# Opening the self attentions in parts between the last passes of the cross attentions

## The reference

```python
x = x + _L0_xattn_ref(_layernorm(x), ctx_512, Wq, Wkv, Wo)        # 16 heads of 16, over the context
x = x + _L0_attn_ref(_layernorm(x), w_attn, b_attn, w_proj, ...)  # causal, 16 heads, over 64 tokens
x = x + _L0_ffn_ref(_layernorm(x), w_gate, w_up, w_down)          # weights rounded to -1, 0, 1
x = x + _L1_xattn_ref(_layernorm(x), ctx_512, ctx_512, ...)       # one head over the context
x = x + _L1_attn_ref(_layernorm(x), W, b)                         # causal, 16 heads, no projection
x = x + _L1_ffn_ref(_layernorm(x), gate_w, ...)                   # 32 experts, top 8, and a shared one
```

## Time and profile before

| | |
|---|---|
| profiled execution, device time | 1285.13 us |
| its span (first to last instruction) | 1283.0 us |
| instructions | 30312 |
| TensorE matmuls busy | 1197.6 us (93%) |
| VectorE, ScalarE, GpSimd busy | 810.0, 643.5, 558.5 us |
| layer 1 ends, layer 2 begins | 250 to 281 us from the start |
| layer 2 ends, feed-forward begins | 400 to 414 us |
| layer 4 ends, layer 5 begins | 564 to 579 us |

### The profile page before, as it was taken

How to read it: one execution, slowest core, us unless ns; L and a number is a source line. 1 busy time by engine, 2 the same in 40 slices (tenths; PEclk the granted TensorE clock), 3 DMA queues, 4 the chain that set the end, 5 groups by cost and what they waited for, 6 DMA issues and landing times.

```text
span 1283.0 us, 30312 instructions
## 1 busy us (share of the span) xinstructions
PE 1197.6 (93%) x9820; PEld 946.3 (74%) x9828; DVE 810.0 (63%) x1773; ACT 643.5 (50%) x1394; POOL 558.5 (44%) x833
## 2 busy tenths in 40 slices
PE   6899999989997777998998999999999999999998
PEld 5677777767775445877776888888888888888886
DVE  4688888757776885658999875444444544444444
ACT  5766666634454786545556443334334433343342
POOL 2244444467775443548887433333233223323322
PEclk9999999989999998999999999999999999999999
DMA  8200000000000000210000133333333343333331
GB/s 286 59 18 16 16 16 8 2 1 2 0 0 18 16 0 10 74 30 14 1 0 1 54 108 120 114 110 106 109 103 114 121 128 103 110 114 114 105 112 62
DMA packets 34041, 80.13 MB, mean 62 GB/s; under 512 B 4416, under 2 KB 12096, under 8 KB 33984
## 3 DMA queue, kind: packets, MB, share of 16 engines
q1 hardware_dynamic: 32800, 78.09, 18.7%
q10 hardware_dynamic: 1184, 1.31, 0.3%
HBM read 77.03 MB, written 2.36 MB: 62 GB/s over the span
## 4 chain that ended last, share of the span: by engine, by line
PE 79%; DVE 7%; issue 5%; ACT 5%; POOL 4%; DMA 0%; ACTq 0%; DVEq 0%; POOLq 0%; SPq 0%
PE ps L2117 10%; PE ps L2119 10%; PE ps L2118 10%; PE ps L2200 5%; PE ps L2199 5%; PE ps L2201 5%; PE ps L421 4%; PE ps L968 3%; PE ps L436 3%; PE ps L409 3%; PE ps L959 2%; PE ps L938 2%; PE ps L975 2%; PE ps L947 2%; POOL Sm L1212 1%
## 5 line engine op out<-in xcount | busy, mean ns | idle before, releaser
L2486 POOL TENSOR_TENSOR sw<-sg,wb 128x512 f32<-128x512 f32 x136 | 176.4, 1297 | 386.7 <-ACT sg L2310 352.8
L2389 DVE TENSOR_TENSOR a<-sw,ps 128x512 f32<-128x512 f32 x136 | 93.5, 687 | 224.8 <-POOL sw L2486 224.5
L2315 ACT ACTIVATE ah<-a 128x512 fp32r<-128x512 f32 x136 | 86.0, 632 | 290.7 <-DVE a L2389 268.5
L2117 PE MATMUL ps<-Hh,wh 128*128 128x512 f32 x544 | 215.3, 396 | 0.0
L2118 PE MATMUL ps<-Hl,wh 128*128 128x512 f32 x544 | 214.4, 394 | 0.0
L2119 PE MATMUL ps<-Hh,wl 128*128 128x512 f32 x544 | 214.4, 394 | 0.0
L2393 DVE TENSOR_TENSOR al<-a,ah 128x512 fp32r<-128x512 f32 x136 | 95.5, 702 | 62.5 <-ACT ah L2315 59.3
L674 ACT ACTIVATE Pr<-ps,mx 128x256 f32<-128x256 f32 x256 | 103.9, 479 | 61.1 <-DVE mx L575 61.1
L2119 PEld LDWEIGHTS ps<-Hh,wl 128*128 128x128 f32 x544 | 101.8, 187 | 25.1
L2117 PEld LDWEIGHTS ps<-Hh,wh 128*128 128x128 f32 x544 | 101.9, 187 | 24.8 <-issue 0.8
L2118 PEld LDWEIGHTS ps<-Hl,wh 128*128 128x128 f32 x544 | 101.9, 187 | 23.6
(11 more groups left out here) (238 smaller groups left out, 2469.1 us busy)
## 6 DMA issues: line engine op xcount, KB each, us to landing
wb<-token_weights SPq DMA_DIRECT2D x64, 512.0 KB, 3.7
raw<-in_ew SPq DMA_DIRECT2D x66, 384.0 KB, 3.0
cT<-in_ctxT SPq DMA_DIRECT2D x16, 256.0 KB, 2.7
cx<-in_ctxT SPq DMA_DIRECT2D x15, 256.0 KB, 2.7
X<-in_x SPq DMA_DIRECT2D x1, 1536.0 KB, 7.2
wqkv<-in_wqkv SPq DMA_DIRECT2D x2, 768.0 KB, 5.1
raw3g<-in_wg SPq DMA_DIRECT2D x1, 1024.0 KB, 5.5
raw3u<-in_wu SPq DMA_DIRECT2D x1, 1024.0 KB, 7.6
```

Source lines behind the costliest of these rows:

```text
L2117: eng.matmul(ps[:, bank, :], wh[:, u, w], HhT[:, c, cols], start=(c == 0), stop=False)
L2389: eng.tensor_tensor(a[:, tt, :], sw[:, tt, :], ps[:, UB[tt], :], ALU.mult).then_inc(m_a, 1)
L2486: eng.tensor_tensor(sw[:, tt, :], sg[:, tt, :], wb[:, u, tt * UT:(tt + 1) * UT], ALU.mult).then_inc(m_sw, 1)
```

## The change

`long_pipeline` and `routed_pipeline` take a `first` and a `finish`, which are generators: they yield `PART` between pieces. `in_turn` changes over between the running block's `finish` and the next block's `first` at each such yield. Computed values and the number of operations stay the same. The rest is order:

- Both cross attentions get a `finish` on each engine, both self attentions a `first`. The first `scores` and the second `qkproj` of the self attention move ahead of the last operations of the cross attention, and `mask(0,0)` ahead of its last `add_x`.
- `opened` is split: each piece waits only for the banks that it uses. In layer 2 the transpose of pair 0 goes to bank 7 (`F0`) instead of bank 3.
- The normalisation of the next block's pair 0 is done in pass 14 (`leading`) instead of 15, in layer 1 and layer 2; so are the two scaled biases.
- GpSimd rounds the last three weight shares (13, 14, 15) in one piece behind pass 14, ahead of the opening.
- In `cross_single`, ScalarE now does `turned(14)`, then the opening's `ln_act`, then `mixed(13)` and `exps(15)`.

```diff
 def in_turn(eng, *layers):
     programs = [layer(eng) for layer in layers]
-    next(programs[0])
+    while next(programs[0]) != MAIN:
+        pass
     for this, following in zip(programs, programs[1:]):
-        next(this)
-        next(following)
+        while next(this) != TAIL:
+            pass
+        mark = next(following)
         for _ in this:
-            pass
+            if mark != MAIN:
+                mark = next(following)
+        while mark != MAIN:
+            mark = next(following)
...
# cross_heads, tensor
+        def finish():
+            i, u, v = NPAIR - 1, 1, 0
+            mix(i - 1, v, 2)
+            turn(i - 1, 7)
+            yield TAIL
+            turn(i, 0)
+            mix(i - 1, v, 3)
+            turn(i, 1)
+            mixed(i - 1)
+            turn(i, 2)
+            scores(i, u, 1)
+            turn(i, 3)
+            mix(i, u, 0)
+            yield PART
+            turn(i, 4)
+            mix(i, u, 1)
+            tail2(i - 1, v)
+            turn(i, 5)
+            tail3(i - 1, v)
+            turn(i, 6)
+            yield PART
+            mix(i, u, 2)
+            turn(i, 7)
+            yield PART
+            mix(i, u, 3)
+            mixed(i)
+            yield PART
+            tail2(i, u)
+            tail3(i, u)
...
# cross_heads, vector: pass 15 as before without the ln_dve calls, then
+            yield TAIL
+            add_x(i - 1)
+            turned(i, 6)
+            yield PART
+            turned(i, 7)
+            yield PART
+            denominators(i)
+            normalise(i, u)
+            yield PART
+            add_x(i)
...
# cross_heads, gpsimd
+            for t in range(NPAIR - 3, NPAIR):
+                quantise(t)
+            yield TAIL
...
# self_heads, tensor
+        def first():
             if layer == 2:
                 eng.wait_ge(s_w1, late)
-                eng.wait_ge(g["c_exp"], 8 * NPAIR)
                 eng.wait_ge(g["c_ke"], 2 * NPAIR)
                 eng.wait_ge(g["c_ve"], 2 * NPAIR)
             else:
+                eng.wait_ge(g["d_qe"], 2 * NPAIR)
+            ln_pe(eng, L, 0, 0, F0)
+            yield PART
+            if layer == 5:
+                eng.wait_ge(g["d_ce"], NPAIR)
+            qkproj(0, 0)
+            yield PART
+            if layer == 2:
+                eng.wait_ge(g["c_exp"], 8 * NPAIR - 1)
+            else:
                 eng.wait_ge(ln_hT, g["lnt"][3] + NPAIR)
-                eng.wait_ge(g["d_qe"], 2 * NPAIR)
-                eng.wait_ge(g["d_ce"], NPAIR)
+            vproj(0, 0)
+            yield PART
+            if layer == 2:
+                eng.wait_ge(g["c_exp"], 8 * NPAIR)
+            ln_pe(eng, L, 1, 1, FH)
+            yield PART
+            if layer == 5:
                 eng.wait_ge(g["d_exp"], NPAIR)
+            scores(0, 0, 0)
+            qkproj(1, 1)
...
# self_heads, vector
+        def first():
+            ln_dve(eng, L, 1, 1)
+            yield PART
+            ln_dve2(eng, L, 1, 1)
+            yield PART
+            v_out(0, 0)
+            yield PART
+            mask(0, 0)
...
# self_heads, scalar
+        def first():
+            eng.wait_ge(s_w1, late)
+            eng.wait_ge(g["s_bq"], 2)
+            ln_act(eng, L, 0, 0, F0)
+            yield PART
+            qk_out(0, 0)
+            yield PART
+            ln_act(eng, L, 1, 1, FH)
...
# cross_single, tensor
+        def finish(body):
+            scores(last, 1, last % R, last // R)
+            mix(last - 2, 1)
+            yield TAIL
+            keys(last, last % R)
+            turn(last - 1, 0)
+            vproj(last - 2, 1)
+            yield PART
+            body(NPAIR, 0, NPAIR // R)
+            yield PART
+            yield PART
+            mix(last, 1)
+            yield PART
+            vproj(last, 1)
...
# cross_single, scalar
+        def finish(body):
+            turned(last - 1, 0)
+            yield TAIL
+            mixed(last - 2, 1)
+            exps(last, 1)
+            yield PART
+            mixed(last - 1, 0)
+            turned(last, 1)
+            yield PART
+            mixed(last, 1)
```

More of the change, by code:

```diff
@@ L55, in opening, with leading @@
     return isinstance(i, int) and i == -1
+def leading(i):
+    return isinstance(i, int) and i == NPAIR - 2
 def closing(i):
@@ L65, in upto, with long_pipeline @@
     return min(n, most) if isinstance(n, int) else n
-def long_pipeline(eng, body, once=None):
-    body(-1, 1, True, False, False, False, 1)
-    yield
+MAIN, TAIL, PART = "main", "tail", "part"
+def long_pipeline(eng, body, first=None, finish=None, once=None):
+    if first:
+        yield from first()
+    else:
+        body(-1, 1, True, False, False, False, 1)
+    yield MAIN
     body(0, 0, True, True, False, False, 1)
@@ L561, in weight_sums @@
             eng.wait_ge(q_sc, 1)
-        yield from long_pipeline(eng, body, weight_sums)
+        yield from long_pipeline(eng, body, finish=finish, once=weight_sums)
     def vector(eng):
@@ L664, in vector @@
         eng.memset(g["epsc"][:, :], EPS).then_inc(s_half, 1)
-        yield from long_pipeline(eng, body, weight_scales)
+        yield from long_pipeline(eng, body, finish=finish, once=weight_scales)
     def scalar(eng):
@@ L992, in body @@
             v = 1 - u
-            if mid:
+            if mid and not known(i, 1):
                 scores(i, u, 0)
@@ L998, in body @@
                 turn(i - 1, v, 1)
[L999 to L1002, removed]
+            if known(i, 1):
                 settled(eng)
-            if front:
+            if front and not known(i, 1):
                 qkproj(i + 1, v)
@@ L1030, in tensor @@
             g["tail5"]["tensor"] = dict(turn=turn, pv=pv)
-        yield from pipeline(eng, body)
+        yield from pipeline(eng, body, first)
     def vector(eng):
@@ L1109, in body @@
                 ln_dve(eng, L, i + 2, u)
-            elif closing(i) and proj:
-                ln_dve(eng, L + 1, 0, v)
-            elif not closing(i) and not proj:
+            elif leading(i) and proj:
+                ln_dve(eng, L + 1, 0, u)
+            elif leading(i):
                 g["first_low"](eng, 0)
@@ L1595, in pairs @@
                 body(R * j + R + r, r, j + 1)
-        for i in range(12, NPAIR):
+        for i in range(12, NPAIR - 1):
             body(i, i % R, i // R)
-        yield
-        for i in range(NPAIR, NPAIR + 3):
-            body(i, i % R, i // R)
+        yield from finish(body)
     def sync(sp):
@@ L1763, in body @@
                 keys_out(i, u)
-        yield from pairs(eng, body)
+        def finish(body):
+            body(last, last % R, last // R)
+            yield TAIL
+            body(NPAIR, 0, 4)
+            yield PART
+            yield PART
+            body(NPAIR + 1, 1, 4)
+            yield PART
+            body(NPAIR + 2, 2, 4)
+        yield from pairs(eng, body, finish)
     def scalar(eng):
```

117 lines of the change are left out of this document (82 added, 35 removed).

## The result

The changed kernel takes 1284.49 us (median of 20 runs, 1280.79 to 1287.15) beside 1287.32 for the kernel before in the same comparison (20 runs). The ratio is 0.9965, with a 95% interval of 0.9952 to 0.9978: 4.5 us less, between 2.8 and 6.2. That ratio is one of means (1288.27 and 1283.75 us); the medians are 2.8 us apart. The sum had said 6.6 us less. The profiled execution took 1282.41 us (span 1280.3), 2.7 less than the one before it.

What follows compares the result with a forecast made beforehand. The prediction took TensorE, busy 93% of the span, as the bound, with waits and half clock at block transitions. Gains 5.5 + 0.8 + 0.3 = 6.6 us from 1286.99 gave 1280.4 us, range 1276.6 to 1284.2.

Steps and rivals of the forecast that it cites:

- The sum: All terms together: 5.5 + 0.8 + 0.3 = 6.6 us less, giving 1280.4 us.
- TensorE's chain of layer 1→2: TensorE's work and remaining waits put layer 2's `scores(0,1)` at 273.8 against 280.77: 7.0 us earlier, the upper end.
- The late chain that decides: Layer 2: last `add_x`, pair 2's statistics, `h`, then second mask at about 276.0 against 281.50; 5.5 us taken as gain.
- Pass 14: Layer 1: the normalisation moved into this pass costs VectorE 0 to 0.1 us.
- Weight slices: GpSimd's last three weight shares, rounded sooner, end near 260; between -0.2 and 0.5 us, taken as 0.
- Layer 4→5: Second mask of layer 5 at 578.4 against 579.19, despite a 1.1 us wait before `vproj(13)`; gain 0.8 us (-1 to 2.6).
- Layer 2→FFN: Layer 2 to feed-forward: last mask no longer waits for GpSimd and rounded `r` comes sooner; gain 0.3 us (0 to 1.0).
- the clock: First transition: about 13.7 us of matmuls in 16, denser than before, so no fall counted on; kept as a risk.
- the clock falls once more: Rival: a fall in one of the merged stretches costs 3 to 4 us, 1283.4 to 1284.4 us; chance 0.18.

Runs made afterwards that it cites:

- e_lns: Changed kernel with pair 2's statistics moved ahead of the cross attention's last `add_x` on VectorE, in both self attentions; 1279.97 us, ratio 0.9931.
- e_qlead: Kernel before with the last three weight shares rounded in one piece and pair 0's normalisation in pass 14, no merging; 1286.98 us, ratio 0.9997.
- e_quant: Kernel before with GpSimd's weight shares 14 and 15 put ahead of the opening of layer 2; 1294.55 us, ratio 1.0045.
- e_first: Changed kernel with only layer 1 to 2 merged, layer 4 to 5 in the order of before; 1284.34 us, ratio 0.9966.
- after: The changed kernel with the whole change, against the kernel before; 1284.49 us, ratio 0.9965.
- e_after2: The changed kernel measured once more, unedited, on another chip than the two half-change runs; 1284.06 us, ratio 0.9968.
- e_second: Changed kernel with only layer 4 to 5 merged, layer 1 to 2 in the order of before; 1291.03 us, ratio 1.0010.
- e_filler: Changed kernel with 13 unread matmuls added on TensorE at layer 2's end and the feed-forward's start; 1279.59 us, ratio 0.9947.
- e_qlate: Changed kernel with weight shares 14 and 15 put back behind the opening of layer 2 on GpSimd; 1286.62 us, ratio 0.9985.
- e_mixed: Changed kernel with ScalarE's old order in layer 4's last pass: `mixed(13)`, `turned(14)`, then the opening; 1280.29 us, ratio 0.9943.
- before: The kernel without the change; 1287.32 us in the comparison with the changed kernel.
- e_lm: Changed kernel with pair 2's statistics sooner and ScalarE's old order in layer 4, no added matmuls; 1276.14 us, ratio 0.9923.
- e_best: Changed kernel with pair 2's statistics sooner, ScalarE's old order in layer 4 and 22 unread matmuls; 1273.72 us, ratio 0.9886.

## Why the prediction came out as it did

- *TensorE's chain of layer 1→2, 7.0 us:* right. `scores(0,1)` was forecast at 273.8 and stands at 273.93. Everything in this profile stands about 0.35 us later than in the one before already two passes ahead of the change (`mix` at 234.86 against 234.52), so counted from `mix(14,2)` it comes 7.2 us sooner. Of the old order the prediction names waits of 0.78 and 0.70 us around the fall of the clock; the one just ahead of that fall (270.0) was longer, 1.35 us, and is gone in the new order:

```profile
268.33 0.63 PE L421 MATMUL ps<-ident,Pr 128*128 128x128 f32 x4 [1.35 <-DVE PT L581]
```

- *The late chain that decides, 5.5 us:* right, step by step. `add_x(15)` 273.2 and 273.30, statistics 273.6 and 273.64, `h` 275.6 and 275.28, mask 276.0 and 275.90. `e_lns` shows it to be what TensorE waits for: without it 1.14 us come back. Counted from `mix(14,2)`, the mask comes 5.96 us sooner and `scores(1,1)` 6.06.
- *Pass 14, 0 to 0.1 us:* right. It lasts 250.00 - 234.86 = 15.14 us, against 15.12 before, so the bias scalings in it cost nothing either.
- *Weight slices, 0:* right in the time (done at 261.4, forecast near 260) and in the value; `e_qlead` has 0.9997. That the order of root and slices could make TensorE wait 3.99 us (`e_quant`) I hadn't seen, only that late slices would.
- *Layer 4→5, 0.8 us:* at full clock 0.66, read in `e_first` against after at the second mask (16.42 and 15.75 us behind layer 4's last scores) and at `turn(0,1)`. The wait for `mixed(13)` was forecast at 1.1 and is 0.92. But the late chain's wait of 1.57 us ends in a fall of the clock (578.29), and up to `scores(1,1)` nothing is left: 23.45 against 23.36. What makes the clock fall here stays open. The wait of 1.57 us stands in six profiles, and in five of them (`after`, `e_after2`, `e_second`, `e_filler`, `e_qlate`) the clock falls at it, but not in `e_mixed`. The old order has no such wait, yet the clock falls near here in `before`, `e_quant` and `e_qlead`, and not in `e_first`. The four profiles with the edit of `e_lns` have no fall here.
- *Layer 2→FFN, 0.3 us:* 0.53 at full clock (135.84 in `e_qlead` against 135.31 in `e_lm`). But the clock cost 5.34 us there in `after` and 4.50 in `e_after2` (against 135.31), where it had cost 1.30 before (137.14 against 135.84).
- *The step that failed: the clock.* "I count on no fall there" held in the first transition. But the speed won back in the second `qkproj` and around it was booked in the 5.5 us as a net gain, and falls were looked for only in the merged stretches. After, the 10.2 us at 1.2 GHz of the first transition are gone, and 2→FFN has 17.1 instead of 3.4. If the 10.2 us had gone for good, the mean clock would be higher by 10.2 x 0.5 / 1283 = 0.004; it is 0.9867 in 88 executions before and 0.9877 in 32 after (standard error 0.0006). At equal clock the change is worth 3.3 us, 2.9 of it in the first transition, so by this estimate about 3 of the 6.06 us were clock. The rival "the clock falls once more" had the right size, 3 to 4 us, and the wrong place.

The Trainium skill ("TensorE: Matmul & The Clock Gate", "HAM oscillation — how this bites in real kernels") lays such falls to long idle waits; the trace shows one after waits of 0.89 us and less (390.97, 394.56, 396.70), so here the measurement decides. Nor do these waits explain it by themselves. The kernel before has the same three, 0.56, 0.69 and 0.88 us, and its clock stays at 1.00 from 396 to 420:

```profile
396.67 0.66 PE L959 MATMUL ps<-Vs,PT 128*64 128x34 f32 x16 [0.56 <-ACT PT L1150]
400.26 0.66 PE L959 MATMUL ps<-Vs,PT 128*64 128x34 f32 x16 [0.69 <-ACT PT L1150]
402.39 0.63 PE L947 MATMUL ps<-ident,Pr 128*128 128x128 f32 x4 [0.88 <-ACT Pr L1145]
```

`e_mixed`, whose instructions up to there are those of `after`, has them too; its clock falls only at 406.5, for 3.4 us. Nor does the fall need the change's order. The fall begins 114.5 to 115.1 us behind layer 2's `scores(1,1)` and lasts 10.2 us in `after`, `e_after2`, `e_first`, `e_second` and `e_qlate`, and also in `e_quant`, whose layer 2 is that of the kernel before. What decides whether it comes stays open: no run changed only what came before. So the link between the fall removed and the fall gained rests on the mean clocks over many executions, not on the two profiles.

So the steps of the order came out within 0.6 us each, and 6.6 forecast and 4.5 measured differ by the clock. The absolute 1284.49 lies 0.3 us above the range's top.

## What to carry to other kernels

When an order removes a stretch at 1.2 GHz, don't book the speed won back as gain until the page's clock row shows that the low clock hasn't moved: compare the time at 1.2 GHz of both kernels, and, since one profile is one draw, the mean clock of many executions and their times at equal mean clock. When a block of work is drawn forward between the last passes of another, look for the instruction of the old work that stands in some engine's order ahead of a statistic or a mask of the new; here drawing that normalisation forward too gave another 1.1 and 1.4 us at the two places. Background work on a slow engine goes where nothing with a due time stands behind it: by their place alone the same shares cost nothing (`e_qlead`), 2.7 us at equal clock (`e_quant`), or 1.8 us in the merged order (`e_qlate`).

## What the runs showed of the hardware

- The clock can fall after short waits, but needn't: in `after` it fell after 0.56, 0.69 and 0.89 us with matmuls between; `before` had the same waits there and stayed at 1.00. With 13 matmuls that nothing reads at these places the mean clock of 12 executions was 0.9920, of 32 without them 0.9877.
- What 1 us at 1.2 GHz costs: about 0.3 us. 2→FFN has 17.1 us of it in `after` and is 5.34 us longer than in `e_lm`, which has none; in `e_after2` it is 13.7 and 4.50.
- These fillers cost nothing that the profile shows: 44 records of 379 ns in `e_best`, and 2→FFN takes 135.32 us with its 13 and 135.31 without (`e_lm`).
- One kernel's times spread over 6 us and more (1280.79 to 1287.15), and most of it is the mean granted clock of the execution: correlation -0.94 in the 20 runs of `after`, 0.7 us for each 0.001. `e_best`, at a mean of 0.998, spreads over 1 us (1273.14 to 1274.10, 4 runs).
